# Local attention of a two-layer block: values stationary for four heads at once, and a new plan

## Chip, cores and metric

One Trainium2 chip, one core. The metric is the device time of one execution in microseconds (us). The kernel before took 2231.11 us as the median of three runs (2227.65, 2231.11, 2232.37).

## The reference

The input is 16 sequences of 256 tokens with 128 features, float32. Two blocks run one after the other, each of the form x = x + A(layernorm(x)) + F(layernorm(x)):

- block 0: A is a selective scan (state of 16, inner size 256), F routes every token to one of 8 experts.
- block 1: A is an attention over 16 heads of 8 features with scores (1 + arccos(cos))^-3.2. F is two layers of **local attention** with 8 heads of 64 features and a feed-forward part. Only the local attention is rewritten here:

```python
# each head: q, k, v of 256 tokens x 64; window 64; a query sees itself and the 64 tokens before it
sim = einsum('bhwid,bhwjd->bhwij', bq, bk)      # q is scaled by 8
sim = where((i < j) | (i > j + WINDOW), -max, sim)
attn = softmax(sim, axis=-1)                    # max, exp, sum
out = einsum('bhwij,bhwjd->bhwid', attn, bv)
x = x + concat_heads(out) @ wo                  # then layernorm, gated GELU feed-forward
```

## The kernel before

The 16 sequences are worked off as 8 pairs (NPAIR) of 512 tokens. Block 1 of pair i runs while the scan (units m_...) of later pairs goes on, so three streams share the engines: the scan (m), the arccos attention (g) and the local layers. A local **step** is one layer (l) of one sequence (b) of one pair: 8 x 2 x 2 = 32 steps. The two sequences of a pair are two independent chains; n = 2 i + l numbers the steps of a chain.

**The planner.** The work is cut into units such as ("score", n, b, k). `all_units` gives each unit a due time and the units that it comes after, `STAGES` and `durations` what it costs on each engine, and `schedule` lists the units greedily into one order per engine, with 8 PSUM banks and a few shared buffers as resources (`takes_banks`, `frees_banks`, `holds`). LATER and STREAM are offsets of the due times. The five engine programs then walk through their orders; an engine runs its list strictly in that order, each unit waiting for semaphores. `into` waits until the unit's bank has been read by its last user.

**A step's attention**, for 256 tokens (two tiles of 128 queries, q-tiles) and 8 heads:

- score k (k = 0..3, two heads, two banks; L1135 to L1151): two bf16 matmuls put the mask (256 columns) in, four matmuls on 64x64 parts of the array add the second q-tile's scores, two on 64x128 parts the first's. VectorE reduces them to the negated maximum per query, nmx (L1684).
- pt k (two heads, two banks; L1152 to L1168): the same scores transposed (keys on partitions): the mask (two bf16 matmuls of 320 columns, L1155), six score products of 128, 128 and 64 columns (L1159), then the negated maximum, broadcast by four float32 matmuls with nmx stationary and the identity moving (L1165 128 columns, L1166 192 columns). ScalarE takes the exponential of 128x640 into PT[k % 2] (L1426); the two PT buffers are shared by both chains (`holds`, `shared_before`).
- pv k (one head; L1169 to L1182): three float32 matmuls with the probabilities stationary and 65 columns moving (64 of values and a column of ones, which gives the row sum). Three heads share a bank.
- on k (three, three and two heads): VectorE takes the reciprocal of the sums (L1694) and multiplies (L1698).
- oT k (q-tile): four transposes each (L815, the helper for all transposes), copied by ScalarE (L1429). Then wo (L1195), the residual, layernorm and the feed-forward part.

A float32 matmul stands in the trace as two MATMUL rows, a transpose and a bf16 matmul as one, each with its LDWEIGHTS row.

```python
LAYER = ("shift qkv0 qkv2 qkv3 qkv5 norm qn0 heads0 qn1 heads1 score0 score1 pt0 pt1 pv0 pv1 pv2 on0 pv3 score2 score3 "
         "pt2 pt3 pv4 pv5 on1 pv6 pv7 on2 oT0 oT1 wo ln ln2 lnT up0 up1 up2 gelu hid0 hid1 hid2 down")
```

Of the kernel before, what the change touches and what calls it, by code (L numbers as in the profile page):

```python
# [6 lines left out]
ALU = mybir.AluOpType  # L7
# [3 lines left out]
P = 128  # L11
# [38 lines left out]
OH = 3  # L50
OG = -(-LH // OH)
# [21 lines left out]
    "g_out": [("PE", 0.89), ("DVE", 0.68)], "out": [("DVE", 0.69), ("SP", 0.1)], "zeros": [("DVE", 0.34)],  # L73
    "shift": [("PE", 0.22), ("ACT", 0.97)], "norm": [("DVE", 0.17), ("ACT", 0.5)], "qn": [("DVE", 1.22)], "heads": [("PE", 0.88), ("ACT", 1.03)],
    "score": [("PE", 1.0), ("DVE", 0.61)], "pt": [("PE", 2.32), ("ACT", 0.7)], "pv": [("PE", 0.64)], "on": [("DVE", 0.78)],
    "oT": [("PE", 0.44), ("ACT", 0.6)], "wo": [("PE", 1.83), ("DVE", 0.42)], "ln": [("PE", 0.69), ("DVE", 0.77), ("ACT", 0.54)],
# [12 lines left out]
         "norm": "ln", "pt": "ln", "ln": "ln", "m_in": "silu", "g_tan": "tan", "gelu": "gelu"}  # L89
SWITCH = 127.0  # L90

LATER = {"down": 9, "e_down": 27, "e_lg": -177, "e_ln": 421, "e_load": -1379, "e_place": 30, "e_pre": -533, "e_route": -824,
         "e_scat": 827, "e_store": -1322, "e_tr": 261, "e_up": 40, "e_xn": -205, "e_xt": -160, "f_ln": 337, "f_tr": -1175,
         "f_xn": 125, "f_yg": 758, "g_av": 86, "g_avT": -766, "g_ev": -1332, "g_hd": -30, "g_ln": 728, "g_norm": -329, "g_oT":
         355, "g_out": 176, "g_pow": 587, "g_qkv": 73, "g_score": 51, "g_sq": 85, "g_sub": 1181, "g_tan": 60, "gelu": -398,
         "heads": 45, "hid": -32, "l_weights": 124, "ln": -103, "ln2": 5, "lnT": -6, "m_B": 636, "m_C": -449, "m_bx": 56,
         "m_dt": 27, "m_du": -6, "m_ex": -11, "m_fin": 286, "m_hc": 82, "m_in": -32, "m_load": 285, "m_out": -1531, "m_scan":
         1342, "m_sum": 17, "m_turn": -313, "m_weights": -862, "m_xp": 1631, "norm": -9, "oT": -3, "on": -102, "out": 152,
         "pt": -29, "pv": 73, "qkv": 47, "qn": -92, "score": -1, "shift": -37, "up": -72, "wo": 32, "x_load": 78, "zeros": 451}

STREAM = {("e", 0): 131, ("e", 1): 87, ("e", 2): 61, ("e", 3): 65, ("e", 4): 580, ("e", 5): 193, ("e", 6): 235,
# [25 lines left out]
def durations(unit):  # L127
# [29 lines left out]
def all_units():  # L157
# [154 lines left out]
    for b in range(2):  # L312
        unit(EARLY - 1, ("zeros", 0, b), ("f_yg", 0))
# [11 lines left out]
def bank_of(unit):  # L325
# [8 lines left out]
    if u == "pv":  # L334
        return ("o", n, b, k // OH)
# [1668 lines left out]
```

## Time and profile before

| quantity | value |
|---|---|
| median of three runs | 2231.11 us (2227.65 to 2232.37) |
| span of the profiled execution | 2227.9 us; its own time is not listed apart from it |
| PE (matmul) busy | 1918.6 us, 86% of the span |
| DVE (VectorE) busy | 1749.3 us, 79% |
| ACT (ScalarE) busy | 1716.7 us, 77% |
| POOL (GpSimd) busy | 606.3 us, 27% |
| mean granted TensorE clock | 0.892 of 2.4 GHz |

PE is the matmuls, PEld the weight loads, which overlap them. Matmuls are pipelined, so the durations of neighbouring matmul rows overlap; what a group of them takes of the engine is the distance from its first start to the next group's first start. The granted clock is a mean over time at 2.4 GHz (1.00) and at 1.2 GHz (0.50). L12 is line 12 of the kernel.

### The profile page before, as it was taken

To read this page: it belongs to the slowest core of one execution; us is meant where nothing else is said; L and a number is where in the kernel's file an instruction comes from. 1 tells how busy PE (TensorE), PEld (TensorE's weight loads), DVE (VectorE), ACT (ScalarE), POOL (GpSimd) and SP (SyncE) were. 2 spreads that over 40 slices of the span, in tenths; PEclk is the share of its full clock that TensorE was granted. 3 is DMA by queue.
4 is the path that set the end of the run, shared out by engine and by line. 5 is a ranking of instruction groups with operands and counts; after the bars stand their busy time and mean duration, and the time that the engine had idled before them with its cause. 6 is when DMAs were issued, how large, how long until landed. Compare 5 with 4: busy or idle time off the path is not lost.

```text
span 2227.9 us, 37707 instructions
## 1 busy us (share of the span) xinstructions
PE 1918.6 (86%) x13746; PEld 1454.8 (65%) x13746; DVE 1749.3 (79%) x2649; ACT 1716.7 (77%) x2817; POOL 606.3 (27%) x272
## 2 busy tenths in 40 slices
PE   3677988989897889898889987899789989899997
PEld 2564766778575667667666666667666767676776
DVE  4889897675899889869976799779987898856553
ACT  2446787838887478897888989887888787897987
POOL 2351222222231033421242223403233132313221
PEclk9788888999998988999888998999889998898989
DMA  7651112442111111011200121011100111000000
GB/s 238 223 181 54 48 57 72 131 144 69 59 63 48 49 44 57 30 40 48 67 17 4 49 62 53 11 53 39 62 11 11 62 54 48 1 1 6 1 1 6
DMA packets 67687, 126.74 MB, mean 57 GB/s; under 512 B 8852, under 2 KB 40276, under 8 KB 67380
## 3 DMA queue, kind: packets, MB, share of 16 engines
q1 hardware_dynamic: 61808, 113.19, 16.2%
q0 software_dynamic: 2816, 7.21, 0.9%
q10 hardware_dynamic: 2884, 3.93, 0.5%
q8 instruction: 114, 1.87, 0.4%
q14 instruction: 65, 0.53, 0.1%
HBM read 111.46 MB, written 12.85 MB: 56 GB/s over the span
## 4 chain that ended last, share of the span: by engine, by line
PE 39%; DVE 25%; issue 17%; ACT 14%; DMA 2%; SPq 2%; POOL 0%; DVEq 0%; another core or an unknown queue 0%; ACTq 0%; POOLq 0%
PE ps L815 6%; DVE hB L1536 5%; PE ps L1063 4%; PE ps L1123 3%; DVE hB L1530 3%; PE ps L1159 2%; DVE hB L1542 2%; PE ps L1195 2%; ACT L810 2%; PE ps L1013 2%; PE ps L1166 2%; PE ps L1165 2%; DVE lss L1659 2%; DVE rb L1666 2%; ACT arena L1374 2%
## 5 line engine op out<-in xcount | busy, mean ns | idle before, releaser
L1823 POOL TENSOR_TENSOR arena<-arena 128x1024 f32<-128x1024 f32 x128 | 345.8, 2724 | 755.9 <-ACT arena L1353 755.8
L1827 POOL TENSOR_TENSOR arena<-arena,rb 128x1024 f32<-128x1024 f32 x64 | 166.2, 2596 | 672.0 <-DVE rb L1666 672.0
L1536 DVE TENSOR_TENSOR_SCAN hB<-dA,hB 128x1024 f32<-128x1024 f32 x128 | 316.7, 2479 | 0.7 <-ACT dA L1312 0.5
L815 PE MATMUL ps<-w_ident,arena 128*128 128x128 f32 x879 | 158.4, 333 | 104.9 <-DVE arena L1469 30.7
L815 PEld LDWEIGHTS ps<-w_ident,arena 128*128 128x128 f32 x879 | 127.5, 173 | 136.3 <-issue 81.2
L1374 ACT ACTIVATE arena<-arena 128x256 f32<-128x256 f32 x512 | 205.4, 402 | 2.0
L1312 ACT ACTIVATE dA<-mv,w_A_log 128x510 f32<-128x510 f32 x256 | 168.5, 712 | 49.3 <-DVE hB L1536 48.6
L1123 PE MATMUL ps<-w_l_wqkv,arena 128*128 128x512 f32 x384 | 196.3, 640 | 10.5 <-DVE nmx L1684 6.2
L810 ACT ACT_TABLE_LOAD x147 | 188.6, 1283 | 15.3 <-issue 12.7
L1530 DVE TENSOR_TENSOR hB<-BC,mv 128x1024 f32<-128x1024 f32 x128 | 189.3, 1483 | 13.8 <-PE ps L1013 10.8
L1607 DVE TENSOR_SCALAR arena<-ps 128x1024 f32<-128x1024 f32 x128 | 155.2, 1217 | 40.6 <-PE ps L1063 40.5
L1542 DVE TENSOR_TENSOR hB<-hB,BC 128x1024 f32<-128x1024 f32 x128 | 186.5, 1458 | 0.4
L1013 PE MATMUL ps<-w_ident,hB 128*128 128x128 f32 x1024 | 153.2, 298 | 34.5 <-DVE hB L1542 33.2
L1063 PE MATMUL ps<-gqT,gkT 8*128 8x256 f32 x1024 | 160.6, 460 | 21.6 <-issue 4.2
L1351 ACT ACTIVATE arena<-arena,one_b 128x2048 f32<-128x2048 f32 x64 | 127.9, 1999 | 64.3 <-DVE arena L1607 59.8
L1013 PEld LDWEIGHTS ps<-w_ident,hB 128*128 128x128 f32 x1024 | 129.6, 156 | 53.6 <-DVE hB L1542 43.9
L1426 ACT ACTIVATE PT<-ps 128x640 f32<-128x640 f32 x128 | 89.1, 696 | 73.7 <-PE ps L1166 55.8
L1684 DVE TENSOR_REDUCE nmx<-ps 128x4 f32<-128x512 f32 x128 | 87.5, 684 | 69.9 <-PE ps L1147 69.7
L1166 PE MATMUL ps<-ident_q,nmx 128*128 128x192 f32 x512 | 132.3, 341 | 0.0
L1063 PEld LDWEIGHTS ps<-gqT,gkT 8*128 8x128 f32 x1024 | 97.4, 212 | 51.3 <-issue 34.9
L1353 ACT ACTIVATE arena<-arena,one_b 128x2048 f32<-128x2048 f32 x64 | 128.2, 2003 | 2.1
L1369 ACT ACTIVATE arena<-arena,one_b 128x2048 f32<-128x2048 f32 x64 | 127.7, 1995 | 0.1
(222 smaller groups left out, 4554.6 us busy)
## 6 DMA issues: line engine op xcount, KB each, us to landing
BC<-bc_d SPq DMA_DIRECT2D x128, 512.0 KB
BC<-in_experts SPq DMA_DIRECT2D x16, 514.0 KB
arena<-in_experts SPq DMA_DIRECT2D x15, 514.0 KB
mv<-in_experts SPq DMA_DIRECT2D x15, 514.0 KB, 3.6
arena<-in_x SPq DMA_DIRECT2D x8, 256.0 KB, 5.6
xnT_d<-arena SPq DMA_DIRECT2D x8, 256.0 KB, 4.9
hB<-xnT_d SPq DMA_DIRECT2D x8, 256.0 KB
x<-in_x SPq DMA_DIRECT2D x8, 256.0 KB, 4.0
```

What stands on the lines that cost most here:

```text
L810: a.preload_act_table_set(names[0])
L815: return t.transpose(out_, in_, ident[0:k, 0:k])
L1013: e = t.matmul(lb()[:, tt * P:(tt + 1) * P], hB[k % 2][:, j, tt * P:(tt + 1) * P], ident, is_transpose=True, start=q == j == tt == 0, stop ...
L1063: e = t.matmul(lb(z)[:, kt * L:(kt + 1) * L], gkT[32 * hi:32 * hi + GD, hb, kt * P:(kt + 1) * P], gqT[32 * hi:32 * hi + GD, hb], start=Tru ...
L1123: e = t.matmul(lb(z), hT1[b][:, tt * P:(tt + 1) * P], w_lqkv[:, l, (w + z) * INNER:(w + z + 1) * INNER], start=True, stop=True)
L1166: e = t.matmul(lb(z)[:, P:SC], top[1], ident_q[:], start=False, stop=True)
L1312: e = a.activation(dA[k % 2][:, j].rearrange("p (s l) -> p s l", s=2)[:, :, 1:], dtv[:, c].rearrange("p (s l) -> p s l", s=2)[:, :, 1:], A ...
L1374: e = a.activation(part, part, ACT.Exp, scale=-3.2, accum_out=vt[m % 2][:, kt, hi, GD + 2:GD + 3])
L1530: v.tensor_tensor(hB[k % 2], Bb[q % 2], bc(du[:, c:c + 1], [P, NG, T]), ALU.mult).then_inc(v_bx, 1)
L1536: v.tensor_tensor_scan(hf, flat2(dA[k % 2]), hf, 0.0, ALU.mult, ALU.add).then_inc(v_scan, 1)
L1542: v.tensor_tensor(hB[k % 2], hB[k % 2], Cb[q % 2], ALU.mult).then_inc(v_hc, 1)
L1823: g.tensor_tensor(la[m % 2][:, half], la[m % 2][:, half], cl[m % 2][:, half], ALU.subtract).then_inc(g_sub, 1)
```

## The change

- **pv** is turned round: the values are stationary (128x32 parts: 32 of a head's 64 features), the probabilities move, and four heads run in the four column quarters of the array. Two units of 16 matmuls replace eight units of three. The result comes out transposed (features on partitions), so **oT** (8 transposes, 2 copies) goes. The order of its features is another one, which the host puts into wo.
- **rsum** is new: two units of 8 matmuls with a column of ones stationary give the row sums of all heads, 32 partitions wide each; after the second, ScalarE computes 1/sum as exp(-ln(sum)) in two activations. **on** becomes two multiplications. The column of ones in vv and its memset (zeros) go.
- **score** uses 64x64 parts throughout: four mask matmuls, eight score matmuls.
- **pt** has two score products a head (192 and 128 columns) in place of three, puts the mask in behind them, and adds the maximum by transpositions of the broadcast nmx (two of 128 columns a head) and one matmul of 64 columns a head.
- Each chain gets PT buffers of its own; PT k is free again when rsum and pv of the same chain have read it.
- rsum's bank is held from rsum 0 until ScalarE has read it after rsum 1; pv 0's bank until on 0, which comes after that reciprocal.
- The planner's costs, LATER and STREAM are new; the arithmetic is otherwise the same. PERIOD and the units of the other streams stay.

```diff
-OH = 3
-OG = -(-LH // OH)
+OH = 4
+OG = LH // OH
+HD = LD // 2
-    "score": [("PE", 1.0), ("DVE", 0.61)], "pt": [("PE", 2.32), ("ACT", 0.7)], "pv": [("PE", 0.64)], "on": [("DVE", 0.78)],
-    "oT": [("PE", 0.44), ("ACT", 0.6)], "wo": [("PE", 1.83), ("DVE", 0.42)], "ln": [("PE", 0.69), ("DVE", 0.77), ("ACT", 0.54)],
+    "score": [("PE", 0.62), ("DVE", 0.61)], "pt": [("PE", 1.7), ("ACT", 0.7)], "rsum": [("PE", 0.65)], "pv": [("PE", 1.15)], "on": [("DVE", 0.66)],
+    "wo": [("PE", 1.83), ("DVE", 0.42)], "ln": [("PE", 0.69), ("DVE", 0.77), ("ACT", 0.54)],
...
+LAYER = ("shift qkv0 qkv2 qkv3 qkv5 norm qn0 heads0 qn1 heads1 score0 score1 pt0 pt1 rsum0 pv0 score2 score3 "
+         "pt2 pt3 rsum1 pv1 on0 on1 wo ln ln2 lnT up0 up1 up2 gelu hid0 hid1 hid2 down")
...
+                        x += [(w, n, b, k // 2 - 1) for w in ("rsum", "pv") if k >= 2]
...
-        PT = [sb(f"PT{k}", [P, 2, SC + WIN])[:] for k in range(2)]
+        PT = [[None, sb(f"PT{b}", [P, 2, SC])[:]] for b in range(2)]
+            PT[b][0] = qf[:, 0:2 * SC].rearrange("p (z c) -> p z c", z=2)
...
                 elif u == "score":
-                        t.matmul(lb(z)[:, 0:SQ], ident_b[:], mask_b[:], start=True, stop=False)
+                        for y in range(2):
+                            t.matmul(lb(z)[head_rows(y), 0:SQ], ident_b[head_rows(z), head_rows(z)], mask_b[head_rows(z), y],
+                                     start=True, stop=False)
...
-                    for z in range(2):
-                        e = t.matmul(lb(z)[:, 0:P], qT[head_rows(z), k, b * L:b * L + P], kT[head_rows(z), k, b * L:b * L + P],
-                                     start=False, stop=True)
+                    for y in range(2):
+                        for z in range(2):
+                            q0 = b * L + y * WIN
+                            e = t.matmul(lb(z)[head_rows(y), 0:P], qT[head_rows(z), k, q0:q0 + WIN], kT[head_rows(z), k, b * L:b * L + P],
+                                         start=False, stop=True)
...
                 elif u == "pt":
-                    for kt, q0, cols in ((0, 0, slice(0, P)), (1, P, slice(P, 2 * P)), (0, P, slice(2 * P, SC))):
+                    for kt, cols in ((0, slice(0, SC - P)), (1, slice(SC - P, SC))):
...
+                    for z in range(2):
+                        t.matmul(lb(z)[:, 0:SC], ident_b[:], maskT_b[:], start=False, stop=False)
                     t.wait_ge(v_mx[b], 4 * n + k + 1)
...
-                        t.matmul(lb(z)[:, 0:P], top[0], ident, start=False, stop=False)
-                        e = t.matmul(lb(z)[:, P:SC], top[1], ident_q[:], start=False, stop=True)
+                        t.matmul(lb(z)[:, 0:P], top[0], ident, is_transpose=True, start=False, stop=False)
+                        t.matmul(lb(z)[:, SC - P:SC], top[1], ident, is_transpose=True, start=False, stop=False)
+                        e = t.matmul(lb(z)[:, P:SC - P], top[1], ident[:, 0:WIN], start=False, stop=True)
...
+                elif u == "rsum":
+                    for kt, cols, q0 in ((0, slice(0, SC - P), 0), (1, slice(SC - P, SC), P)):
+                        for hi in range(OH):
+                            at = k * L + q0
+                            e = t.matmul(lb()[32 * hi:32 * hi + 32, at:at + cols.stop - cols.start], bc(one_b[:, 0:1], [P, 32]),
+                                         PT[b][hi // 2][:, hi % 2, cols], start=k == kt == 0, stop=k == kt == 1, skip_group_check=True)
...
-                    t.matmul(o0, pt[:, 0:P], vv[:, 2 * b, k], start=True, stop=True)
-                    t.matmul(o1, pt[:, P:2 * P], vv[:, 2 * b + 1, k], start=True, stop=False)
-                    t.matmul(o1, pt[:, 2 * P:], vv[:, 2 * b, k], start=False, stop=True).then_inc(p_o[b], 1)
+                    for w in range(2):
+                        for kt, cols, q0 in ((0, slice(0, SC - P), 0), (1, slice(SC - P, SC), P)):
+                            for hi in range(OH):
+                                at = w * L + q0
+                                e = t.matmul(lb()[32 * hi:32 * hi + 32, at:at + cols.stop - cols.start],
+                                             vv[:, 2 * b + kt, OH * k + hi, w * HD:(w + 1) * HD], PT[b][hi // 2][:, hi % 2, cols],
+                                             start=w == kt == 0, stop=w == kt == 1, skip_group_check=True)
...
                 elif u == "pt":
-                    bb, mm = before[unit]
-                    if mm:
-                        a.wait_ge(p_o[bb], mm)
-                    a.activation(PT[k % 2][:, :, 0:SC], two_banks(unit)[:, :, 0:SC], ACT.Exp).then_inc(a_pt[b], 1)
+                    if OG * n + k // 2:
+                        a.wait_ge(p_o[b], OG * n + k // 2)
+                        a.wait_ge(p_rs[b], OG * n + k // 2)
+                    a.activation(PT[b][k % 2], two_banks(unit)[:, :, 0:SC], ACT.Exp).then_inc(a_pt[b], 1)
+                elif u == "rsum":
+                    use(LN_EXP)
+                    a.wait_ge(p_rs[b], OG * (n + 1))
+                    r_ = oT[b].rearrange("p (g w) t -> p g w t", g=OG)[:, :, 1]
+                    a.activation(r_, lb().rearrange("p (g t) -> p g t", g=OG), ACT.Ln).then_inc(a_own, na.up())
+                    a.wait_ge(a_own, na.n)
+                    a.activation(r_, r_, ACT.Exp, scale=-1.0).then_inc(a_rs[b], 1)
...
                 elif u == "on":
-                    v.reciprocal(r_, o_[:, :, :, LD]).then_inc(v_own, nv.up())
+                    v.wait_ge(p_o[b], OG * n + k + 1)
+                    v.wait_ge(a_rs[b], n + 1)
+                    o_ = oT[b][:, 2 * k:2 * k + 2]
+                    v.tensor_tensor(o_, bank(("pv", i, b, k)).rearrange("p (w t) -> p w t", w=2), bc(oT[b][:, 2 * k + 1:2 * k + 2], [P, 2, L]), ALU.mult).then_inc(v_oT[b], 1)
```

## Rows read from the trace of the kernel before

**Rows 1.** The page's first part: busy time, share and instructions of each engine.

```profile
PE 1918.6 (86%) x13746; PEld 1454.8 (65%) x13746; DVE 1749.3 (79%) x2649; ACT 1716.7 (77%) x2817; POOL 606.3 (27%) x272
```

**Rows 2.** Windows: length, busy time of each engine, granted clock, DMA share, GB/s.

```profile
200.00:1900.00 1700.00, 1500.26 (x10908) 1138.12 (x10906) 1415.00 (x2020) 1359.32 (x2183) 450.24 (x178) 0.90 0.17 53
1900.00:2228.00 328.00, 297.87 (x2256) 225.80 (x2254) 185.22 (x344) 277.68 (x454) 83.75 (x35) 0.90 0.01 3
1950.00:1981.00 31.00, 30.93 (x297) 24.37 (x298) 17.68 (x45) 27.29 (x51) 10.33 (x5) 1.00 0.01 1
1995.00:2029.00 34.00, 28.34 (x182) 21.28 (x182) 21.36 (x42) 25.00 (x47) 6.47 (x3) 0.85 0.00 1
```

**Rows 3.** The page's chain that ended last, by engine.

```profile
PE 39%; DVE 25%; issue 17%; ACT 14%; DMA 2%; SPq 2%; POOL 0%; DVEq 0%; another core or an unknown queue 0%; ACTq 0%; POOLq 0%
```

**Rows 4.** Timeline of PE, 1960 to 1973: start, us, line, operands, count.

```profile
1960.28 1.07 PE L1077 MATMUL ps<-arena,vt 128*32 128x256 f32 x16
1961.28 0.44 PE L815 MATMUL ps<-w_ident,xn 128*128 128x128 f32 x2
...
1966.43 0.39 PE L1179 MATMUL ps<-arena,PT 128*128 128x65 f32 x2
...
1967.10 0.43 PE L1155 MATMUL ps<-maskT_b,ident_b 128*128 128x320 bf16 x2
1967.46 0.89 PE L1159 MATMUL ps<-arena 64*128 64x128 f32 x12
1968.28 0.49 PE L1165 MATMUL ps<-w_ident,nmx 128*128 128x128 f32 x2
...
1969.48 0.60 PE L815 MATMUL ps<-w_ident,avS 128*128 128x128 f32 x4
1969.92 0.38 PE L1140 MATMUL ps<-mask_b,ident_b 128*128 128x256 bf16 x2
1970.23 0.45 PE L1144 MATMUL ps<-arena 64*64 64x128 f32 x8
1970.61 0.49 PE L1147 MATMUL ps<-arena 64*128 64x128 f32 x4
1971.03 0.44 PE L1179 MATMUL ps<-arena,PT 128*128 128x65 f32 x2
```

**Rows 5.** Groups by line and form: busy us, mean ns of one, idle before.

```profile
L1077 PEld LDWEIGHTS ps<-arena,vt 128*32 128x32 f32 x1024 | 29.8, 115 | 43.5 <-issue 27.1 <-ACT gqT L1341 2.7 <-ACT arena L1374 2.0
L1698 DVE TENSOR_TENSOR arena<-ps,rs 128x384 f32<-128x384 f32 x64 | 35.7, 558 | 2.2
L1694 DVE RECIPROCAL rs<-ps 128x6 f32<-128x6 f32 x64 | 12.0, 188 | 14.6 <-PE ps L1181 14.3
L1553 DVE TENSOR_TENSOR x<-x,ps 128x512 f32<-128x512 f32 x8 | 5.5, 686 | 13.3 <-PE ps L1029 8.2 <-issue 3.7 <-remote 1.4
L1429 ACT ACTIVATE arena<-ps 128x512 f32<-128x512 f32 x64 | 36.4, 592 | 24.6 <-PE ps L815 24.3
L1298 ACT ACTIVATE hB<-hB 128x512 f32<-128x512 f32 x16 | 10.1, 630 | 0.5
```

**Rows 6.** Waits: who waited for whom, us in total, times, longest.

```profile
PE ps L1155 <- DVE nmx L1684: 7.9, 5, 3.4
PE ps L1140 <- ACT PT L1426: 6.7, 2, 4.0
DVE nmx L1684 <- PE ps L1147: 69.7, 48, 5.3
ACT PT L1426 <- PE ps L1181: 16.9, 9, 4.7
```

**Rows 7.** Timeline of ACT and DVE: one chain's pt 1, pt 3 and last on.

```profile
1946.12 0.70 ACT L1426 ACTIVATE PT<-ps 128x640 f32<-128x640 f32 x1
1960.27 0.68 ACT L1426 ACTIVATE PT<-ps 128x640 f32<-128x640 f32 x1
1972.17 0.42 DVE L1698 TENSOR_TENSOR arena<-ps,rs 128x256 f32<-128x256 f32 x1
```

More of the change, by code:

```diff
@@ L88 @@
 NEEDS = {"e_ln": "ln", "e_route": "ln", "m_weights": "ln", "m_dt": "ln", "m_ex": "ln", "f_ln": "ln", "g_norm": "ln", "g_ln": "ln", "g_pow": "ln",
-         "norm": "ln", "pt": "ln", "ln": "ln", "m_in": "silu", "g_tan": "tan", "gelu": "gelu"}
+         "norm": "ln", "pt": "ln", "rsum": "ln", "ln": "ln", "m_in": "silu", "g_tan": "tan", "gelu": "gelu"}
 SWITCH = 127.0
[L92 to L99, printed above, removed]
@@ L101 @@
-STREAM = {("e", 0): 131, ("e", 1): 87, ("e", 2): 61, ("e", 3): 65, ("e", 4): 580, ("e", 5): 193, ("e", 6): 235,
[13 rows of a table removed]
+LATER = {"down": 9.9, "e_down": -30.3, "e_lg": 99.1, "e_ln": 142.3, "e_load": 49.3, "e_place": 14.3, "e_pre": -1422.1, "e_route": -991.6,
+         "e_scat": 514.1, "e_store": 10, "e_tr": 40.1, "e_up": -5.1, "e_xn": -8.9, "e_xt": -248.5, "f_ln": 517, "f_tr": -404.5,
+         "f_xn": -69.2, "f_yg": -117.1, "g_av": 86.1, "g_avT": -643.8, "g_ev": -328.6, "g_hd": -140.1, "g_ln": 1389.2, "g_norm": -295.4,
+         "g_oT": 281.2, "g_out": 274.1, "g_pow": 830.8, "g_qkv": 63.4, "g_score": 47.3, "g_sq": 67.3, "g_sub": 189.9, "g_tan": 97.5,
+         "gelu": -268.8, "heads": 60, "hid": -81.6, "l_weights": 25.5, "ln": -188.2, "ln2": 4.8, "lnT": -0.9, "m_B": -4.7, "m_C": 577.6,
+         "m_bx": 59.9, "m_dt": 35, "m_du": -135.3, "m_ex": -2.5, "m_fin": 249.3, "m_hc": 90.4, "m_in": -87.6, "m_load": 28.1,
+         "m_out": -177.9, "m_scan": 1803.8, "m_sum": 14, "m_turn": -695.7, "m_weights": 203.9, "m_xp": 1768.8, "norm": 23.7, "on": -309.3,
+         "out": 104.1, "pt": -21.5, "pv": 79.4, "qkv": 39.5, "qn": -53.4, "rsum": 8, "score": -3.8, "shift": -51.3, "up": -103.5,
+         "wo": 139.4, "x_load": -327}
@@ L136, in durations @@
         return [("POOL", 1.5 * TT * (GP[n + 1] - GP[n]))]
+    if u == "rsum" and k:
+        return STAGES[u] + [("ACT", 1.2)]
     if u == "qkv":
@@ L276, in all_units @@
                     elif u == "qkv":
-                        x = [("shift", n, b)] + [("down", n - 1, b) for z in range(1) if n] + [("pv", n - 1, b, 7) for z in range(1) if n and k % 3 == 2]
+                        x = [("shift", n, b)] + [("down", n - 1, b) for z in range(1) if n] + [("pv", n - 1, b, OG - 1) for z in range(1) if n and k % 3 == 2]
                     elif u == "norm":
@@ L347, in takes_banks @@
         return (1, 1)
-    if u == "e_pre" or (u == "e_lg" and n in GP) or (u == "m_sum" and k < CH) or (u == "pv" and k % OH == 0):
+    if u == "e_pre" or (u == "e_lg" and n in GP) or (u == "m_sum" and k < CH) or u == "pv" or (u == "rsum" and k == 0):
         return (0, 1)
@@ L365, in frees_banks @@
         return (-1, ("av", n, b, k))
+    if u == "rsum" and k:
+        return (1, ("r", n, b))
     if u == "on":
-        return (-1, ("o", n, b, k))
+        return (-1, ("pv", n, b, k))
     if u == "ln2":
@@ L386, in holds @@
         takes[2], frees[3] = ["rb"], ["rb"]
-    if u == "pt":
-        takes[1] = [f"PT{k % 2}"]
-    if u == "pv" and k % 2:
-        frees[0] = [f"PT{k // 2 % 2}"]
     return takes, frees
@@ L521, in shared_before @@
     table = {}
-    slot, rb = [(0, 0), (0, 0)], (0, 0)
-    for unit in order(plan, "ACT"):
-        u, n, b, k = unit
-        if u == "pt":
-            table[unit] = slot[k % 2]
-            slot[k % 2] = (b, LH * n + 2 * k + 2)
+    rb = (0, 0)
     for unit in order(plan, "DVE"):
@@ L885, in gpsimd_setup @@
                 g.memset(vt[k][:, :, :, GD + 1:GD + 2], 1.0).then_inc(g_set, 1)
-            for k in range(2):
-                g.memset(PT[k][:, :, SC:], 0.0).then_inc(g_set, 1)
-        all_set = 10
+        all_set = 8
         def vector_setup():
@@ L1986, in constants @@
     q0 = np.arange(P)[None]
-    for name, ahead in (("mask", (m0, m1)), ("maskT", (q0 - i, q0 - i, q0[:, 0:WIN] + P - i))):
-        d_ = np.concatenate(ahead, 1)
+    rows = np.concatenate([np.arange(WIN), np.arange(WIN)])
+    scores = np.concatenate([m0, m1], 1)
+    mask = np.concatenate([scores[rows], scores[rows + WIN]], 1)
+    for name, d_ in (("mask", mask), ("maskT", np.concatenate([np.arange(SC - P)[None] - i, q0 - i], 1))):
         r[name] = np.where((d_ < 0) | (d_ > WIN), np.float32(NEG), np.float32(0)).astype(np.float32)
```

106 lines of the change are left out of this document (37 added, 69 removed), and 25 rows, old and new, of the table STREAM.

## The prediction

> **What bounds the kernel now.** I read the page's busy times first: PE is busy for 1918.6 us of 2227.9, DVE for 1749.3 and ACT for 1716.7 [rows 1]. No engine is full and none is far behind. The chain that ended last says the same: 39% PE, 25% DVE, 14% ACT, 17% issue [rows 3]. So work taken from PE returns less than its own length, since the two others stand 8 or 9 points behind. The windows tell where. From 200 to 1900 us, where scan, arccos attention and local layers overlap, PE is busy for 1500.3 of 1700 us (88.3%), DVE for 1415.0 (83.2%), ACT for 1359.3 (80.0%). From 1900 on the scan is over: PE 90.8% of 328 us, ACT 84.7%, DVE 56.5% [rows 2]. The reader is to see that DVE comes next in the first stretch and ACT in the second.
>
> The profiled execution's own time is not listed, so I make the sum against its span, 2227.9 us, and add at the end the 3.2 us by which the median (2231.1) stands above it.
>
> **What a step costs PE now.** The stretch 1950 to 1981 runs at granted clock 1.00 (2.4 GHz) with PE never idle [rows 2], so distances between starts there are prices at full clock [rows 4].
> - Score: 1969.92 to 1971.03, 1.11 us: masks 0.31, 64x64 part 0.38, 64x128 part 0.42.
> - pt: 1967.10 to 1969.48, 2.38 us: masks 0.36, scores 0.82, maximum 1.20.
> - pv: one head 1966.43 to 1967.10, 0.67 us, so 0.112 us per row of six.
> - Four transposes: 1969.48 to 1969.92, 0.44 us, 0.11 each.
> - The pattern that the new pv takes, 32 columns wide in four column quarters: L1077, 16 rows of 256 columns in 1.00 us (1960.28 to 1961.28). Four quarters run side by side: 256 columns twice at 2.4 GHz are 0.213 us for two of a matmul's four passes, four such groups 0.85, and 0.15 are left for going into and out of this form.
> - Such a change of form shows inside the score unit too. Two masks of 256 bf16 columns stream for 2 x 0.107 = 0.21 us at 2.4 GHz, yet the 64x64 part begins 0.31 after the unit's start: 0.1 between forms. The 64x64 part takes 0.38 where its two groups of 128 columns stream for 0.21: 0.17 more, of which 0.1 is the next change and the rest the first weight load.
>
> **The change on PE, per step, at full clock.**
> - Score k: the masks run in four parts at once, 0.11 in place of 0.22 (plus 0.05 for the first load); eight products of 128 columns are four groups of 0.107 plus a little (0.12), 0.48; entry and exit 0.18 (0.1 each, less what the load above covers). Together 0.82, against 1.11: 0.29 saved, times 4 = 1.2 us.
> - pt k: three products a head become two of 192 and 128 columns. The two heads run side by side, so that is 2 x 0.16 + 2 x 0.107 = 0.53 and, for the forms, 0.24: scores 0.77 in place of 0.82. The masks (2 x 0.133) move behind them and are 0.32 with their first load, against 0.36; changes of form are as many. The maximum: 4 transposes at 0.11 and two 64-column matmuls, four rows, at 0.112, the load-bound price of pv's 65 columns: 0.44 + 0.45 = 0.89 + 0.05, against 1.20. Together 2.03, so 0.35 saved a unit, times 4 = 1.4 us.
> - pv, oT and rsum: 8 x 0.68 + 2 x 0.44 = 6.3 us go. Coming: one group of 192 columns is 0.16, one of 128 is 0.11, so an rsum is 2 x (0.16 + 0.11) = 0.54 and a pv twice that, 1.08; with 0.15 for the form each, 0.69 and 1.23. Twice both: 3.8; where rsum and pv stand together 3.5. I take 3.7: 2.6 saved.
>
> That is 5.2 us a step. Over 32 steps 166 us at full clock, and at the granted 0.90 of both long windows [rows 2] 185 us of PE time. Bounds: if every new unit pays 0.2 for its form and the quarters don't pack better than 64x64 now, 4.4 us a step (156 us). The upper bound is the diff's own cost table: its old entries (1.0, 2.32, 0.64, 0.44) lie at my rows, and its new ones give 19.3 - 12.9 = 6.4 us a step, 228 us. I stay with what rows show.
>
> **The change elsewhere.** DVE: three reciprocals (0.188) and three multiplications (0.558, the last shorter) are 2.1 us a step; two of 128x512 out of PSUM like L1553 (0.686) are 1.37 [rows 5]: 0.7 saved, 23 us in all. ACT: two copies of 0.592 against a logarithm (0.592 to 0.63) and an exponential (0.630, L1298) [rows 5]: even, at worst 3 us more. New on ACT is that rsum needs the ln/exp table; pt and norm beside it need it too, so I price that at nothing; if a reload came with it, one in two steps, that is 16 x 1.3 = 20 us. The loading of a mask twice as wide at the start, the missing copies and the missing memset: within 1 us, no less than a gain of 0.5. What is queued behind the new waits: on ACT, pt 2 now waits for rsum 0 and pv 0 of its chain (1.9 us of PE work, placed before score 2), where before it waited for any chain's pv: that old wait cost 16.9 us in 9 places [rows 6] and largely goes. on 0 waits for pt 3, rsum 1 and 1.2 us of ACT; but oT's round trip PE, ACT, PE goes, so the chain gets shorter. SP's and POOL's lists keep their units, in a new order.
>
> **The sum.** PE gets 185 us less, DVE 23, ACT nothing. The last 328 us hold 6 of the 32 steps (24 of L1426's 128 units), the stretch before them 26. *Tail:* PE 298 - 6 x 5.8 = 263 us. With PE at 90.8% as now it would take 290 us; ACT, 278 + 1, can't go below 279 and at 90.8% takes 307. Between 21 and 38 saved, I take 25. *Middle:* PE 1500 - 151 = 1349, DVE 1415 - 18 = 1397, ACT 1360. If DVE can be kept at the 88.3% that PE has now, 1582 us, 118 saved; if DVE stays at 83.2%, 1679, 21 saved; DVE's largest idle is a wait for score's matmuls (69.7 us) [rows 6], which start sooner now. Three engines at equal load fill worse than one leading: I take 86.5%, 1615, 85 saved. Total 110 us: 2227.9 - 110 = 2118, plus 3 = 2121; that PT buffers no longer couple the chains I put at 6 us, near a third of the 16.9. **Forecast 2115 us**, DVE and PE both near 82 to 83% of the span.
>
> **Rivals.**
> - *The whole gain comes through* (13%): PE stays the bound and keeps its idle time. For it: DVE and ACT idle mostly on PE. Against: DVE would have to stand at 85% on average. 2231 - 185 = 2046 us; with the upper bound down to 2003.
> - *The others don't follow* (12%): DVE's share stays at 83% in the middle (21 us) and the tail gives 21: 2231 - 42 = 2189. A falling clock leads there too: with PE at 82% busy and more gaps, a mean of 0.88 in place of 0.90 stretches 1733 us of PE by 39 us. For it: from 1995 to 2029, where PE is busy for 28.3 of 34 us, the granted clock is 0.85 [rows 2].
> - *Slower by banks* (5%): rsum's and pv 0's banks are held from pt 1 to the first on. In the trace that is 1946.1 to 1972, 26 us [rows 7], two banks in each of two chains; before, a bank was held for three heads only. Where m_sum holds two banks and g_av one, three are left for pairs, and PE stands in `into`. Now PE's waits for a bank read late are small (the two largest are 7.9 and 6.7 us in all [rows 6], 0.5 us a step). The point where it decides is 185 / 32 = 5.8 us more per step; at 7.5 it adds 240 and the time is 2231 - 185 + 240 = 2286 us.
> - *Quarters don't hide their weight loads* (1%): a step has 96 loads of 128x32, 0.115 us each [rows 5]. If they stood in line, they would be 11.0 us where I take 3.7, so 7.3 more than my 5.2 saved: 2.1 us a step the other way, 32 x 2.1 / 0.90 = 75, 2306 us. Against it: L1077's 16 loads would be 1.84 us and its unit takes 1.00 [rows 4, 5]. The Trainium skill ("TensorE: Matmul & The Clock Gate", Part 3, what overlaps and what doesn't) says that loads overlap running matmuls only where their row groups differ, and all of these use the same rows; by that rule this rival would be the outcome. The measured unit contradicts it, and the measurement decides.
> - *It does nothing measurable* (3%): PE's saved time all becomes waiting. 2231 us; about 0.2% is what a measurement of this kernel can tell from no change.
>
> **Chances.** Forecast 66%, the others as given. Faster by over 0.2%: 66 + 13 + 12 = 91%; within 0.2%: 3%; slower: 6%. The range takes in the forecast with its bounds (middle at 88.3% and tail at 38 give 2075; PE's upper bound some 30 us more) and most of the second and part of the first rival: 2045 to 2180 us.
>
> **What would show it.** In the profile after: PE busy near 1733 us, DVE near 1725, ACT within 20 us of 1717. A pt unit 2.0 us from start to start at clock 1.00, a score unit 0.8, rsum 0.55 to 0.7, pv 1.1 to 1.25. DVE's largest waits still on PE, but shorter. If pt is 1.7 us, the table was right and PE falls below 1700. If PE's waits for banks (a unit's first matmul behind ACT's or DVE's reads of another unit) sum to over 100 us, the bank rival is at work. I am wrong about the mechanism if PE falls by over 180 us and the span by less than 50, or if the span falls by more than PE.

## The result: 1.3% slower, with 174 us less work on PE

The kernel with the change takes 2262.57 us (median of four runs, 2257.62 to 2267.43), the kernel before beside it 2231.68: ratio 1.0134, 95% interval 1.0103 to 1.0165. Forecast were 2115 us and the range 2045 to 2180; slower had 6%. The profiled execution took 2257.62 us, its span is 2256.2 us at a mean granted clock of 0.865 (before 2227.9 at 0.892).

The first part of the page after the change (it answers to [rows 1]):

```profile
PE 1777.2 (79%) x15282; PEld 1283.1 (57%) x15282; DVE 1758.6 (78%) x2517; ACT 1737.6 (77%) x2830; POOL 610.2 (27%) x270
```

PE's busy time fell by 141.4 us. Multiplied by the mean clock, its work at full speed fell from 1918.6 x 0.892 = 1711 to 1777.2 x 0.865 = 1537 us, by 174; the sum said 166. (The product is an estimate: the clock is a mean over the span, not over the time in which PE was busy.) But the span grew by 28.3, so PE's idle time rose from 309.3 to 479.0 us. The windows after the change, in the columns of [rows 2]:

```profile
200.00:1900.00 1700.00, 1378.40 (x12105) 997.49 (x12104) 1426.96 (x1913) 1372.68 (x2179) 456.58 (x177) 0.87 0.17 52
1900.00:2256.00 356.00, 278.79 (x2594) 196.28 (x2592) 181.41 (x320) 283.68 (x469) 86.11 (x36) 0.86 0.01 3
```

PE dropped from 88.3% to 81.1% in the long stretch, yet DVE only went from 83.2% to 83.9% and ACT from 80.0% to 80.7%. No other engine came under load in PE's place: over the whole span each of the three stands idle for a fifth of the time or a little more.

Where did the local steps go? Windows of ACT for the exponential of pt alone (its line; 128 of them in all), cut near the times at which the kernel before had started 32, 64, 96 and all 128. One that runs across a cut is counted on both sides, which is why the counts of before add up to 131. First the kernel before, then the changed one:

```profile
200.00:745.00 545.00, 21.80 (x32) 0.90 0.25 75
745.00:1260.00 515.00, 22.12 (x33) 0.89 0.13 42
1260.00:1771.00 511.00, 22.51 (x33) 0.90 0.13 40
1771.00:2201.00 430.00, 22.02 (x33) 0.91 0.05 15
```

```profile
200.00:745.00 545.00, 22.32 (x32) 0.88 0.24 74
745.00:1260.00 515.00, 21.53 (x31) 0.88 0.13 43
1260.00:1771.00 511.00, 21.55 (x31) 0.85 0.13 40
1771.00:2201.00 430.00, 20.86 (x30) 0.86 0.04 14
```

The columns are the window, its length, ACT's busy time on that line (count), granted clock, DMA share and GB/s. A local step takes over 5 us less of PE, and still the steps come no sooner: 32, 31, 31 and 30 per window against 32, 33, 33 and 33. At 2201 us, when the last one of the kernel before has started, the change has four of the 128 still to come.

**The new units cost what the sum said, or less.** Timeline of PE after the change, 1145 to 1157, at clock 1.00 (columns as in [rows 4]):

```profile
1145.41 0.82 PE L1152 MATMUL ps<-arena 64*128 64x192 f32 x8
1146.16 0.45 PE L1155 MATMUL ps<-maskT_b,ident_b 128*128 128x320 bf16 x2
...
1147.22 1.05 PE L1003 MATMUL ps<-w_ident,hB 128*128 128x128 f32 x8
...
1149.26 0.36 PE L1173 MATMUL ps<-arena,one_b 128*32 128x192 f32 x2
...
1149.94 1.09 PE L809 MATMUL ps<-w_ident,arena 128*128 128x128 f32 x8
...
1154.81 0.33 PE L1185 MATMUL ps<-arena 128*32 128x192 f32 x2
...
1156.01 0.30 PE L1131 MATMUL ps<-mask_b,ident_b 64*64 64x256 bf16 x4
...
1156.68 1.07 PE L1067 MATMUL ps<-arena,vt 128*32 128x256 f32 x16
```

From start to next start, with the forecast in brackets: pt 1.81 (2.03), rsum 0.68 (0.69), pv 1.20 (1.23), score 0.67 (0.82). Over all pt units at clock 1.00 most take 1.81, or 1.90 where a score unit follows. A step then takes 4 x 0.67 + 4 x 1.81 + 2 x 0.68 + 2 x 1.20 = 13.7 us, or 14.0 with 1.90; the sum had 3.3 + 8.1 + 3.7 = 15.1.

Six waits of PE that grew: who waited for whom, total, times, longest.

```profile
PE ps L809 <- DVE gpad L1603: 32.5, 22, 5.0
PE ps L1067 <- DVE vt L1623: 24.4, 9, 4.8
PE ps L1201 <- DVE xd L1699: 20.0, 9, 12.6
PE ps L1067 <- ACT arena L1374: 19.7, 5, 6.5
PE ps L1152 <- DVE nmx L1688: 15.0, 8, 5.2
PE ps L1173 <- ACT PT L1426: 14.7, 9, 3.6
```

The first, the second and the fourth belong to the arccos attention, whose units were not changed; before, they were 7.4, 5.0 and 1.9 us. With the same units in another order (e5 below) they are 9.6, 13.8 and 3.9 us, so their length depends on the order.

### The profile page after: what moved, and what is told of

Read it like the earlier page. It is cut to its first block, busy times and chain, and to the rows that moved or that the text cites. A ratio compares the mean times of both kernels' runs of the same rounds, so it can differ in the third digit from the quotient of the medians.

```text
span 2256.2 us, 40273 instructions
## 1 busy us (share of the span) xinstructions
PE 1777.2 (79%) x15282; PEld 1283.1 (57%) x15282; DVE 1758.6 (78%) x2517; ACT 1737.6 (77%) x2830; POOL 610.2 (27%) x270
## 4 chain that ended last, share of the span: by engine, by line
PE 18%; ACT 14%; DVE 14%; issue 8%; DVEq 0%; ACTq 0%
ACT arena L1374 3%; DVE hB L1540 3%; PE ps L1053 2%; PE ps L809 2%; ACT L804 2%; ACT arena L1369 2%; PE ps L1067 2%; PE ps L1113 2%; PE ps L1152 1%; DVE hB L1546 1%; ACT arena L1359 1%; DVE hB L1534 1%; DVE lss L1663 1%; DVE rb L1670 1%; DVE arena L1611 1%
## 5 line engine op out<-in xcount | busy, mean ns | idle before, releaser
L1814 POOL TENSOR_TENSOR arena<-arena 128x1024 f32<-128x1024 f32 x128 | 365.4, 2876 | 656.3 <-ACT arena L1353 656.3
L1818 POOL TENSOR_TENSOR arena<-arena,rb 128x1024 f32<-128x1024 f32 x64 | 158.5, 2477 | 817.2 <-DVE rb L1670 817.2
L1540 DVE TENSOR_TENSOR_SCAN hB<-dA,hB 128x1024 f32<-128x1024 f32 x128 | 330.5, 2589 | 0.9 <-ACT dA L1312 0.5
L1053 PE MATMUL ps<-gqT,gkT 8*128 8x256 f32 x1024 | 169.1, 462 | 41.9 <-DVE arena L1611 13.6
L809 PE MATMUL ps<-w_ident,arena 128*128 128x128 f32 x623 | 115.4, 336 | 84.1 <-DVE arena L1473 31.6
L809 PEld LDWEIGHTS ps<-w_ident,arena 128*128 128x128 f32 x623 | 91.1, 175 | 110.5 <-issue 67.5
L1152 PE MATMUL ps<-arena 64*128 64x192 f32 (+1 forms) x1024 | 120.6, 360 | 38.4 <-DVE nmx L1688 15.0
L1351 ACT ACTIVATE arena<-arena,one_b 128x2048 f32<-128x2048 f32 x64 | 127.9, 1998 | 23.2 <-DVE arena L1611 14.0
L1152 PEld LDWEIGHTS ps<-arena 64*128 64x128 f32 x1024 | 94.2, 213 | 76.8 <-issue 38.0
L1113 PEld LDWEIGHTS ps<-w_l_wqkv,arena 128*128 128x128 f32 x384 | 72.7, 207 | 102.6 <-issue 89.9
L1353 ACT ACTIVATE arena<-arena,one_b 128x2048 f32<-128x2048 f32 x64 | 128.2, 2003 | 2.1
```

Source lines behind the costliest of these rows:

```text
L809: return t.transpose(out_, in_, ident[0:k, 0:k])
L1053: e = t.matmul(lb(z)[:, kt * L:(kt + 1) * L], gkT[32 * hi:32 * hi + GD, hb, kt * P:(kt + 1) * P], gqT[32 * hi:32 * hi + GD, hb], start=Tru ...
L1113: e = t.matmul(lb(z), hT1[b][:, tt * P:(tt + 1) * P], w_lqkv[:, l, (w + z) * INNER:(w + z + 1) * INNER], start=True, stop=True)
L1152: t.matmul(lb(z)[:, cols], kT[head_rows(z), k, at:at + P], qT[head_rows(z), k, at:at + cols.stop - cols.start], start=kt == 0, stop=False)
L1540: v.tensor_tensor_scan(hf, flat2(dA[k % 2]), hf, 0.0, ALU.mult, ALU.add).then_inc(v_scan, 1)
L1814: g.tensor_tensor(la[m % 2][:, half], la[m % 2][:, half], cl[m % 2][:, half], ALU.subtract).then_inc(g_sub, 1)
```

## The experiments

The theory to be tested: the units are as cheap as forecast, and the order of the units, which LATER and STREAM set, throws the gain away. Against it stood: the cost table with which the list was made is wrong (pt 1.7 where 1.81 to 1.90 is measured); banks and coupled chains cost more than PE saves; the clock, lower by 0.027, takes the gain. The span of a list by the kernel's own planner is given beside each run as "list"; it was 2232.9 for the kernel before and 2261.8 for the change. The planner stands in both sources, so these two numbers could be had before anything ran on the chip, and both come within 2 us of the measured times (2231.7 and 2262.6), though for other lists below the planner is up to 35 us off. The prediction did not use them.

### Half the change at the order of before

e1 keeps the order of before and takes in only the score unit of 64x64 parts and the maximum by transposition; e7 only the latter.

```diff
-                        t.matmul(lb(z)[:, 0:P], top[0], ident, start=False, stop=False)
-                        e = t.matmul(lb(z)[:, P:SC], top[1], ident_q[:], start=False, stop=True)
+                        t.matmul(lb(z)[:, 0:P], top[0], ident, is_transpose=True, start=False, stop=False)
+                        t.matmul(lb(z)[:, P:2 * P], top[1], ident, is_transpose=True, start=False, stop=False)
+                        e = t.matmul(lb(z)[:, 2 * P:SC], top[1], ident[:, 0:WIN], start=False, stop=True)
```

> The kernel before with its order of units untouched (same costs, LATER and STREAM), but with the new score unit (64x64 parts throughout) and the maximum added by transpositions; the three products a head, pv, on and oT stay. By my rows that takes 0.33 + 0.27 us a score/pt pair, 2.4 us a step, 77 us of TensorE work at full clock off an order that was made for the dearer units. Theory O (the change lost by its order, TensorE work is worth its time where the order is held): 2185 to 2205 us, 25 to 45 us faster. Theory W (TensorE work is worth nothing, VectorE and ScalarE bound): within 5 us of 2231. Theory S (the new pv's waits and banks cost the time): same as O here, since none of them is in this kernel.

> The kernel before, order untouched, only the maximum in pt added by transpositions (four rows of 0.11 us and four of 0.112 in place of four of 0.112 and four of 0.165): 0.23 to 0.27 us a unit, 30 to 35 us of TensorE work at full clock. It splits the run with both parts, which gained 4 us for 77 us of work while the granted clock fell from 0.892 to 0.865. Theory C1 (transpositions lower the granted clock by themselves): clock 0.87 or lower and no gain. Theory C2 (the clock falls with TensorE's idle time, whatever it runs): clock between 0.87 and 0.89, time within 5 us of the kernel before, about half of what both parts did.

e1: 2235.07 us, ratio 0.9981 (0.9955 to 1.0007). e7: 2240.31, ratio 1.0029 (1.0005 to 1.0052). The pages' first lines, e1 and then e7:

```profile
PE 1883.8 (84%) x14514; PEld 1439.1 (64%) x14514; DVE 1745.0 (78%) x2647; ACT 1715.4 (77%) x2817; POOL 605.3 (27%) x272
```

```profile
PE 1923.9 (86%) x13746; PEld 1449.9 (64%) x13746; DVE 1745.3 (78%) x2649; ACT 1718.0 (76%) x2817; POOL 604.8 (27%) x272
```

In the profiled executions e1 has 1711 - 1883.8 x 0.865 = 81 us less PE work at full speed and e7 43 us less. The time of e1 can't be told from that of before (at most 0.45% shorter by the interval), that of e7 is slightly longer. So theory O missed here: it wanted 25 to 45 us from e1, and what came is what theory W foretold, PE work worth nothing. The profile of e1 says where the 81 us went: PE's busy time fell by only 35 us, since the clock fell from 0.892 to 0.865, and its idle time rose by 49 (309 to 358). With the order held, saved work became waiting and a lower clock. What speaks against W is further down: orders in which the same DVE and ACT work is done in 2157 us (e5).

The last window of e7 and the same window of the kernel before (columns of [rows 2]):

```profile
1900.00:2158.00 258.00, 237.47 (x1719) 175.76 (x1718) 160.10 (x275) 212.98 (x357) 66.55 (x27) 0.86 0.01 2
```

```profile
1900.00:2158.00 258.00, 240.18 (x1813) 178.34 (x1811) 160.75 (x278) 222.66 (x354) 72.78 (x31) 0.92 0.01 2
```

PE is as busy in both (92 and 93%), and the granted clock is 0.86 in one and 0.92 in the other. The order is the same and the idle time nearly (325 us against 309 in all); what differs is that 256 float32 matmuls of 128 columns and as many of 192 became 512 transpositions and 256 matmuls of 64 columns. It is the window with the largest difference; in the four windows from 200 to 1900 e7 is 0.01 to 0.04 lower. Over all runs e7's clock is 0.867 to 0.877, that of before 0.883 to 0.896: the two don't touch. By the expectations the mean of 0.871 lies between C1 (0.87 or lower) and C2 (0.87 to 0.89), and the time, 7 us longer, fits C1, so e7 alone does not decide; e4 and e8, which take the transpositions out at two other orders, raise the clock both times.

### More work at the order of the change

e4 keeps the order of the change and makes its four transpositions a unit regular float32 matmuls, some 56 us more at full speed.

```diff
-                        t.matmul(lb(z)[:, 0:P], top[0], ident, is_transpose=True, start=False, stop=False)
-                        t.matmul(lb(z)[:, SC - P:SC], top[1], ident, is_transpose=True, start=False, stop=False)
+                        t.matmul(lb(z)[:, 0:P], top[0], ident, start=False, stop=False)
+                        t.matmul(lb(z)[:, SC - P:SC], top[1], ident, start=False, stop=False)
```

> The changed kernel with its order untouched, but its four transpositions a pt unit made regular matmuls again (two rows of 0.11 us in place of one): 0.44 us a unit, 128 units, 56 us more TensorE work at full clock. Theory O: at a held order part of it shows, 15 to 40 us: 2278 to 2303 us. Theory W: under 5 us, 2262 to 2267. Theory S: TensorE waits anyway, under 15 us.

2285.12 us, ratio 1.0208 (1.0163 to 1.0252), at a clock of 0.876 to 0.882: 22.5 us above the change by the medians, 17 by the ratios. The two intervals just overlap, so the size is rough: some 56 us of PE work cost some 20, inside theory O's 15 to 40. Transpositions lower the clock (0.858 to 0.866 with them), but here they cost less than what they replace.

### The same disturbance for both

e2 adds the same random offsets, some 3 us each, to every entry of LATER in both kernels.

```diff
-LATER = {"down": 9, "e_down": 27, "e_lg": -177, "e_ln": 421, "e_load": -1379, "e_place": 30, "e_pre": -533, ...
+LATER = {'down': 5.5, 'e_down': 23.6, 'e_lg': -175.0, 'e_ln': 414.1, 'e_load': -1379.4, 'e_place': 23.2, 'e_pre': -529.7, ...
```

> The kernel before, each unit kind's due time moved by a random offset of about 3 us (normal), nothing else: the same work, the same dependencies, another order. Theory O: an order that was not tuned for exactly these costs is worth 4 to 5%, so 2320 to 2350 us. Theories W and S, by which the order matters little: within 1% of 2231, under 2255 us.

> The changed kernel with the same random offsets added to its LATER. Theory O: it loses less than the kernel before does, since its own order is less finely tuned: 2285 to 2310 us, so 30 to 60 us faster than the kernel before under the same disturbance. Theory S: the changed kernel stays slower than the kernel before by its 30 us under the same disturbance, 2350 us or more.

Before moved: 2334.44 us, ratio 1.0416 (1.0372 to 1.0461), list 2342.2. Change moved: 2295.29, ratio 1.0246 (1.0203 to 1.0288), list 2295.1. Offsets of 3 us, in a table that has entries of over 1000, cost the kernel before 97 us (against its runs beside it) and the change 33 (25 by the ratios). Both lie in theory O's ranges. The 2231 us of the kernel before belong to one finely set order; with the same offsets on both, the new structure is 39 us faster. This is one draw of offsets; how far other draws would spread was not measured.

### New orders for the change

LATER and STREAM were searched anew with the kernel's own planner as the measure: e5 with the cost table as it is, e6 with the measured costs (score 0.68, pt 1.93, rsum 0.68, pv 1.2, on 0.69), e11 by another search that starts from the change's own offsets. No unit is altered.

```diff
-LATER = {"down": 9.9, "e_down": -30.3, "e_lg": 99.1, "e_ln": 142.3, "e_load": 49.3, "e_place": 14.3, "e_pre": -1422.1, "e_route": -991.6,
+LATER = {"down": -11537.1, "e_down": -2060.5, "e_lg": -30.3, "e_ln": -3001.3, "e_load": 6528.7, "e_place": 578.9, "e_pre": -10312.0,
...
```

> The changed kernel with other LATER and STREAM offsets, found by a longer random search with the kernel's own planner; its costs and every unit are as in the changed kernel. The planner's list ends at 2192 us with them, against 2262 with the offsets of the change and 2233 for the kernel before. Theory O (the change lost by the order it was given): 2185 to 2205 us, 60 us or more below the changed kernel and 25 to 45 us below the kernel before. Theory S (waits and banks of the new pv can't be ordered away on the chip): 2240 us or more. Theory W: 2230 to 2240, no better than the kernel before.

> As the run before, but the planner's costs of score, pt, rsum, pv and on are set to what the trace of the changed kernel shows (0.68, 1.93, 0.68, 1.2 us on TensorE, 0.69 on VectorE, where the change has 0.62, 1.7, 0.65, 1.15, 0.66), and the offsets are searched for those. The planner's list ends at 2219 us. If wrong costs of the plan were what lost time, this one beats the run before although its list is longer; by theory O it comes out at 2205 to 2230 us, near its list.

> The changed kernel with a third set of offsets, from the changed kernel's own by another search; the list ends at 2190 us, 2 us before that of the 2157 us run. It tells how far equal lists differ on the chip, and may be the fastest version. Theory O: 2145 to 2190 us. Theory S: 2240 us or more.

| kernel | list | time, us | ratio to before (95%) |
|---|---|---|---|
| e5 | 2191.8 | 2157.29 | 0.9653 (0.9632 to 0.9674) |
| e6 | 2219.1 | 2193.64 | 0.9823 (0.9804 to 0.9842) |
| e11 | 2189.9 | 2192.43 | 0.9790 (0.9746 to 0.9834) |

The page's first line of e5, its long window, and the windows of its exponentials, cut as above:

```profile
PE 1728.2 (80%) x15282; PEld 1254.2 (58%) x15282; DVE 1744.6 (81%) x2517; ACT 1715.4 (79%) x2816; POOL 624.1 (29%) x270
```

```profile
200.00:1900.00 1700.00, 1393.82 (x12602) 1008.81 (x12601) 1463.64 (x1975) 1414.06 (x2275) 487.49 (x187) 0.89 0.17 53
```

```profile
200.00:745.00 545.00, 22.33 (x32) 0.91 0.27 82
745.00:1260.00 515.00, 23.71 (x34) 0.88 0.12 37
1260.00:1771.00 511.00, 23.62 (x34) 0.88 0.13 41
1771.00:2201.00 430.00, 19.50 (x28) 0.90 0.05 15
```

With the same units, e5 is 105 us faster than the change (2262.57 to 2157.29; 4.7% by the ratios) and 3.5% faster than the kernel before. DVE stands at 86.1% and ACT at 83.2% in the long window, where the change had 83.9 and 80.7; the exponentials run at 34 and 34 a window, and all 128 are done by 2201 us. All three orders beat the change by more than 3%; e5 came out 28 us below theory O's range, e6 11 below its range, and e11 2 above it. The cost table was not the cause: e5 has the same table as the change. (e6, with the measured costs, is slower than e5, but one search each can't tell the costs from the luck of the search.) The banks and the two chains are used by the same rules in all three, so by themselves they can't hold the change at 2262. The clock is 0.873 to 0.883 in e5 against 0.858 to 0.866, and 0.865 against 0.88 is 30 us of PE's 1777. It does not go by PE's busy share alone: e5 and e11 are both at 80% in their profiled executions, with 0.883 and 0.869.

What these runs don't show is how much of the 105 us the same search would bring the kernel before from its own offsets. That was not tried; the next section compares the two at equal effort from a rougher start.

The planner's span is a guide and no more. On the chip e5 stands 35 us below it, e6 25 below, e11 3 above.

### The same search for both

e9 and e10 start from the two moved lists of e2 and get the same search over the same length of time; e12 gives the same to e1's units (score 0.67 and pt 2.12 in the cost table).

```diff
-LATER = {'down': 5.5, 'e_down': 23.6, 'e_lg': -175.0, 'e_ln': 414.1, 'e_load': -1379.4, 'e_place': 23.2, 'e_pre': -529.7, ...
+LATER = {"down": -23.9, "e_down": 1066.4, "e_lg": -3527.7, "e_ln": 3108.1, "e_load": -6585.4, ...
```

> The kernel before, its offsets first disturbed as in the earlier run (2334 us) and then searched anew for 800 s with its own planner; the list ends at 2273 us. With its partner, the changed kernel treated in exactly the same way, it compares the two structures at equal effort of planning. Theory O: 2255 to 2285 us, above the kernel before's 2232, whose own order is the product of a longer search, and 60 to 80 us above its partner. Theory S: no more than 20 us above its partner.

> The changed kernel, disturbed by the same offsets (2295 us) and searched anew for the same 800 s; the list ends at 2204 us. Theory O: 2165 to 2205 us. Theory S: 2240 us or more.

> The kernel before with two parts of the change, the new score unit and the maximum by transposition (pv, oT, on and PT buffers stay as before), its list made anew: the offsets of the moved list of before, then the same search over LATER and STREAM as its replanned list had; score and pt stand in the cost table with 0.67 and 2.12. The list ends at 2222.5 by the planner's own costs (with the units of before 2272.6, of the change 2204.4; on the chip those were 2289 and 2220 us). Theory (the order decides how much of the saved work shows; at a list of its own the saved 80 us of PE work count by about a half): 2225 to 2255 us, so that score and maximum bring 35 to 65 of the 70 us. Rival A (the parts on the score side bring nothing since DVE's reduction and ScalarE's exponential stand behind them, the gain is all in the turned pv and the missing oT): 2275 to 2295. Rival B (the lists' ends are true to the chip): 2222 plus at most 10.

| units | list | time, us | ratio to before (95%) |
|---|---|---|---|
| of before (e9) | 2272.6 | 2289.24 | 1.0241 (1.0199 to 1.0283) |
| new score and maximum (e12) | 2222.5 | 2236.47 | 0.9997 (0.9970 to 1.0024) |
| of the change (e10) | 2204.4 | 2219.62 | 0.9922 (0.9898 to 0.9946) |

The pages' first lines, e9, e12, e10:

```profile
PE 1940.1 (85%) x13746; PEld 1461.9 (64%) x13746; DVE 1761.5 (77%) x2649; ACT 1734.4 (76%) x2830; POOL 612.3 (27%) x272
```

```profile
PE 1864.2 (83%) x14514; PEld 1413.4 (63%) x14514; DVE 1740.9 (78%) x2647; ACT 1733.7 (78%) x2829; POOL 610.1 (27%) x272
```

```profile
PE 1753.5 (79%) x15282; PEld 1273.1 (57%) x15282; DVE 1721.3 (78%) x2517; ACT 1735.9 (78%) x2830; POOL 612.3 (28%) x270
```

At equal effort the whole structure is worth 70 us for 187 us less of busy PE: 37%. Theory O's ranges were missed on both sides, by 4 us (e9, 2255 to 2285) and 15 us (e10, 2165 to 2205); that e10 is over 20 us faster than e9 speaks against theory S. Score and maximum bring 53 of the 70 for 76 us, the turned pv 17 for 111. All of this rests on one list for each kernel, and equally long lists came out 35 us apart on the chip (e5 and e11). By that measure the direction of the 70 stands, but its size may be anything from 35 to 105, and the 17 from nothing to 50.

### The maximum by matmul at the best order

e8 is e5 with the maximum by regular float32 matmuls of 128 and 192 columns.

```diff
-                        t.matmul(lb(z)[:, 0:P], top[0], ident, is_transpose=True, start=False, stop=False)
-                        t.matmul(lb(z)[:, SC - P:SC], top[1], ident, is_transpose=True, start=False, stop=False)
-                        e = t.matmul(lb(z)[:, P:SC - P], top[1], ident[:, 0:WIN], start=False, stop=True)
+                        t.matmul(lb(z)[:, 0:P], top[0], ident, start=False, stop=False)
+                        e = t.matmul(lb(z)[:, P:SC], top[1], ident_q[:], start=False, stop=True)
```

> The fastest run so far (2157 us, order untouched), with the maximum added by regular float32 matmuls of 128 and 192 columns as in the kernel before, in place of transpositions: 0.32 us a unit, 41 us more TensorE work at full clock. Theory C1 (transpositions lower the granted clock): the clock rises from 0.877 to 0.89 or more, which gives back 20 to 25 us of busy time on 1730, and the time is within 10 us of 2157. Theory C2 (the clock follows idle time alone): the clock rises by less than 0.006 and the time by 15 us or more.

2179.0 us, ratio 0.9733 (0.9678 to 0.9788): 22 us slower than e5 (0.8% by the ratios), for some 41 us more work at full speed and at a clock of 0.883 to 0.893 against 0.873 to 0.883. The time fits C2 (15 us or more), the clock, up by 0.009 on the mean, lies between C1's and C2's. At this order the transpositions pay, net of the clock that they cost. e5 stays the best version measured.

## Why the prediction was wrong

**The step that failed** is in the sum, at "Middle": "If DVE can be kept at the 88.3% that PE has now ... I take 86.5%, 1615, 85 saved", and at "Tail" with "With PE at 90.8% as now". These shares are those of an order of units, and the diff replaces that order: "The planner's costs, LATER and STREAM are new" stood in the change, and the sum has no term for it ("in a new order" is said of SP and POOL alone). What the runs showed in its place: the order alone moves the changed kernel between 2157 and 2295 us (138 us; e2, e5) and the kernel before between 2231 and 2334 (103 us; e2), where the sum had 110. The miss of 138 us between the span of 2256 and the 2118 of the sum divides at 1900 us, by which time both kernels have started nearly the same number of exponentials (104 before, 103 after). The middle took 1700 us where the sum had 1615, so 85 over: DVE did 1427 us of work there for the 1397 forecast, at 83.9% where I took 86.5%. The tail took 356 us for 303, 53 over, with PE busy for 78.3% (278.79 of 356). Why this one order is poor, unit by unit, was not found out. The range had no term for that, and no rival had it either; the only case on the slow side with a chance above 1% was banks.

Point by point:

- *PE's work* was right: 174 us against 166 at full speed. The bounds of 156 to 228 are at the granted 0.90, which is 141 to 205 at full speed. The unit prices give more, 20.3 - 14.0 = 6.3 us a step or some 200 us; the two ways of counting differ by some 26 us, and which is nearer stays open. Score saves more than forecast (0.67 for 0.82), pt too (1.81 to 1.90 for 2.03); rsum, pv within 0.03. The diff's cost table was too low for pt (1.7), as the sum said.
- *PE busy near 1733*: 1777. At the forecast clock of 0.90 the 1537 us would be 1708; the clock was 0.865.
- *The clock* was assumed to stay at 0.90. The transpositions account for a good part of its fall (e7: 0.891 to 0.871 at the same order; e4: 0.8625 to 0.879 on the means when they are taken out of the change). The rest was not traced; PE's larger idle time is the likely one. The rival that named a falling clock had 0.88 and only for gaps.
- *DVE near 1725*: 1758.6. The multiplications are as forecast (row below, 682 ns for 686), but the scan took 2589 ns each for 2479 before, 14 us in all. It is not the change's arithmetic: with the same units the scan takes 2409 ns in e10, where DVE is at 1721.3. What stretches it was not tried.
- *ACT within 20 us of 1717*: 1737.6, 21 more. The priced-at-nothing reload came after all: 160 table loads for 147, 13 x 1.283 = 16.7 us, close to the 20 given for one in two steps. With e5's order there are 146, with e10's again 160. So this too depends on the order.
- *Banks*: the mark was over 100 us of PE waiting for banks. The first matmuls of score and pt units wait 70 us in all after the change, 27 before and 38 in e5 (their rows summed). With the first matmuls of the projections and the arccos scores, and all that these wait for, it is 138 us against 58 before, so the mark is reached; but it was badly set, since it took nothing off for the kernel before, and e5 is over it too (106) and is 105 us faster. The growth is some 80 us, 2.5 a step where 5.8 would decide. Late reads are a part of how a poor order costs, not a limit of the structure.
- *Quarters don't hide their weight loads* falls too: pv's 32 loads of 115 ns (row below) would be 3.7 us in a row and its unit takes 1.20. The Trainium skill ("TensorE: Matmul & The Clock Gate", Part 3) lets loads overlap running matmuls only where row groups differ; the trace contradicts it here, for all these loads use the same rows.
- *The others don't follow* (2189 us) came nearest in mechanism: engines did not take up PE's idle time. But it priced that at a DVE share of 83% and still a gain; it had no way to end above 2231.
- *Own criterion*: "wrong about the mechanism if PE falls by over 180 us and the span by less than 50". PE's busy time fell by 141, its work by 174, the span rose. By the letter neither reaches 180, but the case is the one that it describes. What was wrong is the conversion of work into time, not the work.

Rows of the changed kernel by line and form, for the points above (columns of [rows 5]):

```profile
L1694 DVE TENSOR_TENSOR arena<-ps,arena 128x512 f32<-128x512 f32 x64 | 42.1, 682 | 16.9 <-ACT arena L1433 14.3 <-PE ps L1185 2.5
L1185 PEld LDWEIGHTS ps<-arena 128*32 128x32 f32 x1024 | 58.1, 115 | 29.5 <-issue 18.6
L804 ACT ACT_TABLE_LOAD x160 | 205.3, 1283 | 20.6 <-issue 17.8
L1540 DVE TENSOR_TENSOR_SCAN hB<-dA,hB 128x1024 f32<-128x1024 f32 x128 | 330.5, 2589 | 0.9 <-ACT dA L1312 0.5
```

Would the sum have been right under a good order? e5's 2157 lies inside the range, 42 us above the forecast. Its PE is busy for 1728.2 us (forecast 1733) and DVE's share in the long window is 86.1% (I took 86.5%). What is left over is PE's idle time, 430 us where 2118 - 1733 leaves 385. That PE's busy time comes out so near is in part luck: it had more work taken off than forecast and ran at 0.883 where 0.90 was assumed. And 2157 was found by a search that the change had not had, so it does not make the forecast for the change right.

## What to carry to other kernels

Where engines follow a list made out beforehand, the busy shares read from a trace belong to that list; a diff that replaces it must be priced with a range for the order, and here that range (100 us and more) was as wide as the whole gain. Where the planner is at hand, run it first: its span was within 35 us of the chip for every list tried, and it had the change slower than the kernel before (2261.8 against 2232.9). To judge a new structure, give old and new the same effort of planning or the same disturbance, and compare those: one tuned point against one less tuned point says little of either. And once three engines stand within ten points of each other, don't count on the work saved on the leading one coming through: here it was 37% in the one comparison at equal effort, and nothing that could be told from zero with the order held (e1).

## What was not expected of the hardware

- Transpositions in place of matmuls lower the granted clock at the same order and the same busy share: 0.92 to 0.86 in the last window above, 0.891 to 0.871 over the execution. The Trainium skill ("TensorE: Matmul & The Clock Gate", Part 4) says that transpose mode doesn't count as busy in the same way for the clock; the trace agrees. They pay at two orders, where matmuls in their place cost 22 us (e8) and some 20 us (e4), and not at that of before, where they made it 0.3% longer (e7).
- A 64x64 part of the array packs better than the sum had it: a score unit of 12 matmuls in 0.67 us where 0.82 was worked out from the neighbouring forms.
- Offsets of 3 us in one table made the kernel before 4.2% slower (interval 3.7 to 4.6) with every instruction the same, only their order changed (e2).
